# One wait ahead of GpSimd's result scatters, in a cross-attention and top-1 expert kernel

## The reference

```
x = x + tanh(g_xattn) * attention(layernorm(x), ctx, ctx, mask)      # 16 heads of 64
n = layernorm(x)
idx = argmax(softmax(n @ Wg + bg))                                    # one of E = 8 experts
h = gelu(n @ W1[idx] + b1[idx]);  y = h @ W2[idx] + b2[idx]           # 256 -> 256 -> 256
x = x + tanh(g_ffn) * y
```

## Time and profile before

| | |
|---|---|
| median of three timed runs | 210.49 us |
| span of the profiled execution, first to last instruction | 216.8 us |
| the profiled execution's own time | the profile gives its span alone |
| TensorE (PE) matmuls busy | 196.8 us, 91% |
| VectorE (DVE), ScalarE (ACT), GpSimd (POOL) busy | 125.5, 105.5, 89.5 us |
| mean granted TensorE clock | 0.965 |
| scatters to `out` (line 596) | 16, 996 ns mean |
| sort scatters (line 581) | 8, 1006 ns mean |

### The profile page before, as it was taken

The page is one execution under the profiler, slowest core; times in us unless marked ns, Lnnn a source line. Parts: engine busy times, 40 slices in busy tenths (PEclk is TensorE's granted clock), DMA queues, the critical chain, the costliest instruction groups (busy, mean ns, idle before and its releaser), DMA issues.

```text
span 216.8 us, 3994 instructions
## 1 busy us (share of the span) xinstructions
PE 196.8 (91%) x1262; PEld 144.4 (67%) x1262; DVE 125.5 (58%) x526; ACT 105.5 (49%) x377; POOL 89.5 (41%) x129
## 2 busy tenths in 40 slices
PE   7899899799999999999997999989999996399940
PEld 7644576567765546888956667758889994289930
DVE  3896755998893321443279999887343450145420
ACT  3232618799994213022187999976312451135410
POOL 7000632577579600000007997689100057433460
PEclk9999999999999999999999999999999999559995
DMA  5993589999998001900000106000000014520011
GB/s 135 348 385 129 173 315 323 307 287 300 236 216 266 6 0 38 347 1 0 5 0 25 52 26 196 5 0 3 2 0 0 0 52 128 145 72 17 31 52 21
DMA packets 21505, 25.16 MB, mean 116 GB/s; under 512 B 1939, under 2 KB 19805, under 8 KB 21344
## 3 DMA queue, kind: packets, MB, share of 16 engines
q1 hardware_dynamic: 19456, 22.51, 35.2%
q0 software_dynamic: 1152, 2.12, 2.9%
q10 hardware_dynamic: 864, 0.15, 0.4%
HBM read 14.14 MB, written 11.68 MB: 119 GB/s over the span
## 4 chain that ended last, share of the span: by engine, by line
PE 78%; DVE 8%; ACT 5%; issue 4%; DMA 1%; POOL 1%; POOLq 0%; DVEq 0%; ACTq 0%
PE s_bank L1606 13%; PE o_bank L1561 13%; PE s_bank L1906 7%; PE o_bank L1689 7%; PE o_bank L1917 7%; PE t_bank L1663 7%; PE s_bank L1646 6%; PE s_bank L1715 4%; ACT probs L779 4%; PE o_bank L1682 4%; PE s_bank L1895 2%; PE t_bank L1697 2%; DVE probs L1249 1%; PE t_bank L1579 1%; DVE pT L1270 1%
## 5 line engine op out<-in xcount | busy, mean ns | idle before, releaser
L617 POOL TENSOR_TENSOR probs<-probs,r_col 128x512 f32<-128x512 f32 x32 | 33.4, 1043 | 62.1 <-DVE r_col L1260 61.7
L779 ACT ACTIVATE probs<-probs,negm_run 128x160 f32<-128x160 f32 x128 | 53.0, 416 | 5.1 <-DVE negm_run L1249 5.0
L1249 DVE CUSTOM_DVE_ANT_0 probs<-s_bank,maskneg 128x160 f32<-128x160 f32 x128 | 33.2, 318 | 5.8 <-PE s_bank L1646 5.6
L1606 PE MATMUL s_bank<-xnT,wq_sb 128*128 128x512 f32 x64 | 28.8, 598 | 0.5 <-ACT xnT L728 0.5
L1561 PE MATMUL o_bank<-wo_sb,oT 128*128 128x256 f32 x128 | 28.6, 379 | 0.0
L1561 PEld LDWEIGHTS o_bank<-wo_sb,oT 128*128 128x128 f32 x128 | 23.9, 190 | 3.5 <-issue 0.5
L779 ACT ACTIVATION_READ_ACCUMULATOR probs<-probs,negm_run 128x1 f32 x128 | 24.0, 187 | 0.0
L596 POOL DMA_INDIRECT out_dram<-oT x16 | 15.9, 996 | 15.8 <-DVE oT L1198 13.4
L1646 PE MATMUL s_bank<-k_sb,q_sb 64*128 64x160 f32 x256 | 22.3, 311 | 0.0
L1646 PEld LDWEIGHTS s_bank<-k_sb,q_sb 64*128 64x128 f32 x256 | 17.9, 186 | 4.8 <-issue 4.0
L1606 PEld LDWEIGHTS s_bank<-xnT,wq_sb 128*128 128x128 f32 x64 | 11.7, 190 | 13.6 <-issue 13.5
(11 more groups left out here) (155 smaller groups left out, 296.8 us busy)
## 6 DMA issues: line engine op xcount, KB each, us to landing
sorted_rows<-empty_row SPq DMA_DIRECT2D x8, 1040.0 KB, 14.9
oT<-in_L_ffn_W_dram SPq DMA_DIRECT2D x1, 2048.0 KB, 20.0
q_sb<-in_L_ffn_W_dram SPq DMA_DIRECT2D x1, 2048.0 KB, 8.3
oT<-sorted_rows SPq DMA_DIRECT2D x1, 1040.0 KB, 5.4
oT<-sorted_rows SPq DMA_DIRECT2D x8, 130.0 KB, 2.0
wq_sb<-in_L_xattn_Wq_dram SPq DMA_DIRECT2D x2, 512.0 KB, 6.1
mask_sb<-in_mask_BxSxS_bk_dram SPq DMA_DIRECT2D x2, 512.0 KB, 7.1
wk_sb<-in_L_xattn_Wk_dram SPq DMA_DIRECT2D x1, 1024.0 KB, 11.0
```

Source lines behind the costliest of these rows:

```text
L617: nc.gpsimd.tensor_tensor(window_wide(u), window_wide(u), r.rearrange("p i h -> p (i h)") .unsqueeze(2).broadcast_to([P, 4, WIDE]), ALU.mu ...
L779: last = nc.scalar.activation(window_part(u, i, h), window_part(u, i, h), ACT.Exp, bias=negm_run[at], scale=-1.0, accum_out=l_run[at])
L1249: nc.vector.tensor_tensor_reduce(window_part(u, i, h), s_bank[u % 2][:, h, i * CK:i * CK + WK], maskneg[:, q, 0:WK], -SCALE, LARGEST, ALU. ...
L1606: last = nc.tensor.matmul(bank[m % 4], wq_sb[:, c, m * P:(m + 1) * P], xnT[:, c, b * N:(b + 1) * N], start=(c == 0), stop=(c == DC - 1))
```

## The change

More of the change, by code:

```diff
@@ L668, in rest @@
                     scatter(QT + q)
+                pool.wait_ge(experts[1].s_rows[E // 2 - 1], 16)
                 for e in range(E):
```

## The result

The changed kernel takes 213.34 us in the median of four runs (212.84 to 213.72); the kernel before takes 210.48 (210.47 to 210.69, four runs). The ratio is 1.0134, with a 95% interval of 1.0118 to 1.0150: 2.9 us slower. The forecast was 213.0 in a range of 210.4 to 214.8.

The account below looks back on a forecast made before the run. Without the stall, GpSimd's delayed queue was taken to end the changed kernel: last scatter at 205.75 plus 6.5 us gives span 212.2, plus none to all of 1.6 us unexplained; middle 213.0 us, range 210.4 to 214.8.

Parts of the forecast that it names:

- The stall isn't in the timed runs: Late signals and halved clock between passes, from about 181 us; timed runs, 6.3 us below the profiled span, lack it.
- When the wait ends: GpSimd's hold before its first result scatter ends when read 3 of the second pass lands, at 185.6.
- The price of sharing: Second-pass reads beside result scatters: read 3 took 2.7 us against 2.0 alone.
- First scatter: GpSimd's first result scatter starts 0.77 after the wait, at 186.4 instead of 179.90: 6.5 us late.
- The queue of sixteen: GpSimd's result scatters, 1.29 us each: the ninth at 196.7, the sixteenth at 205.75 against 202.4, 3.4 us more.
- What follows the last scatter: Kernel end: 6.5 us from the last scatter's start to the span's end, giving a span of 212.2.
- Around the span: Unexplained time outside the span or left of the stall: between none and 1.6 us, the middle taken.
- What is gained: Start of pass two: reads 0 to 3 have the DMA engines alone; some tenths at most, nothing in the sum.
- My two bounds on its landing: Read 3 of the second pass lands between 185.5 and 186.5.
- The rival built on it (205.9 us): Between the passes: the stall is in the timed runs too and the wait removes it, 205.9 us; chance 0.12.
- Absorbed: Pass two comes late enough that GpSimd's last scatter falls where it did: same time, 210.5 us; chance 0.07.
- The stall moves: Sixteen back-to-back scatters bring the 7.9 us of stall into pass two: 217.6 us; chance 0.04.

Follow-up runs that it names:

- second trace of the kernel before: The kernel before, unchanged, profiled once more for a second look at its trace: 211.02 us, span 209.3, no stall.
- the kernel with the wait after four: Kernel before plus the wait for read 3 of the second pass, placed after four of GpSimd's eight first-pass scatters: 210.75 us, ratio 1.0004.
- The five kernels with the wait moved or the queue cut: Kernel before plus wait for: read 0, 1.0017; read 7, 1.0328; read 3 after four scatters, 1.0004; after two, 1.0008; with half the first-pass scatters omitted, 0.9978.
- the wait for read 7: Kernel before plus a wait for the second pass's last chunk read, ahead of all scatters to the output: 217.37 us, ratio 1.0328.
- the wait for read 0: Kernel before plus a wait for the second pass's first chunk read, ahead of all scatters to the output: 211.07 us, ratio 1.0017.

## Why the prediction was right

*The stall isn't in the timed runs.* Right. I inferred it from 6.3 us that could lie nowhere else; the second trace of the kernel before and the spans of its 46 timed runs show it directly. Without the stall I had put the last scatter at 202.4 and the span at 208.9; the median 210.48 less 1.74 is 208.7.

*When the wait ends.* 185.6 was predicted and it was 185.94: the two turns took 2.20 and 2.12 us, not 2.0 each. The 2.0 came from a single read of the stalled trace, the one issued at 188.32, between two scatters; it was a little too low. The price of sharing that I took from that trace (2.7 us for read 3) was too high: in the second trace of the kernel before read 3 took from 183.85 to 186.10, 2.25 us, and 2.5 in the kernel with the wait after four.

*First scatter.* 186.4 predicted, 186.72 measured; the 0.77 after the wait was 0.78.

*The queue of sixteen.* Right: scatter 9 at 197.09 (196.7 predicted), scatter 16 at 206.12 (205.75), pitch 1.29. The five kernels with the wait moved or the queue cut show it as the cause: the loss comes with the queue and goes with it.

*What follows the last scatter.* This term was mis-sized. I carried over 6.5 us; it was 211.6 - 206.12 = 5.5. It is why the time grew by 2.3 us between the two clean traces (211.02 to 213.34) though the last scatter moved by 3.3. The trace shows where the 1.0 us went: the last scatter landed 3.0 us after its issue and not 4.0. Why it landed sooner stays open (last section).

*Around the span.* I took 0.8, half of what was open; it is 1.74. The errors are +0.4 (late scatters), -1.0 (tail) and +0.9 (around), and the sum came out 0.3 short of the measured 213.34. The path and its waits were right; that the sum is this near is luck, since two errors of about a microsecond each cancel.

*What is gained.* The "some tenths" from read 2 can't be told from the spread: pass two starts 0.35 us sooner than in the one clean trace of the kernel before, but so it does in the kernel with the wait after four. Whatever it is, it is lost behind GpSimd in the change.

The rule of the Trainium skill, page "DMA: Bandwidth & Descriptors", section "Queues, rings and completion order", that the DMA engines take turns between queues, agrees with the traces as far as they go: read 3 took 2.1 us alone and 2.25 and 2.5 beside scatters, a small share. (My two bounds on its landing were 1.0 us apart; the 0.9 in the prediction counts from the 185.6 that I took.) The other rule, page "Runtime: NRT & Kernel Launch", section "The launch sequence", would have put 6.2 us between profile and reported time whatever the kernel. The page speaks of the profile's total time, which no run here gives. For the span the traces don't bear it out: time less span is +1.74 in the changed kernel and +1.7 in the second trace of the kernel before. The rival built on it (205.9 us) fell.

*The rivals on the other side.* "Absorbed" fell since pass two isn't late. "The stall moves" fell: none of the eight later traces has a stall, with up to sixteen scatters back to back beside pass two. My argument against it had a wrong reading, though: I wrote that nothing was late until hidden 7. In the first trace of the kernel before ScalarE's gelu 6 is late already, by 1.0 us (its line there, then in the changed kernel):

```profile
180.50 0.62 ACT L881 ACTIVATE k_sb<-s_bank,b1T 128x128 f32<-128x128 f32 x2 [1.57 <-PE s_bank L1906]
```

```profile
179.55 0.63 ACT L882 ACTIVATE k_sb<-s_bank,b1T 128x128 f32<-128x128 f32 x2 [0.52 <-PE s_bank L1907]
```

Hidden 6 ended at 178.35 + 1.06 = 179.41 there. So the stall began before the first scatter to `out` (179.90) and before SyncE's reads of pass two (181.12), and neither can have started it. The sort scatters that ran at that time ran alike in the eight traces without a stall.

## What to carry to other kernels

A wait in an in-order queue has to be priced by the queue behind it: count what is left to issue, multiply by its pitch, and set it against the moment at which its last item is needed. Here 6.8 us of hold met 3.5 us of slack; two items moved ahead of the wait took almost the whole loss away. The sum gives how late the last item is issued; the time grew by somewhat less, since what followed the last item got shorter. Compare a profile's span with the timed runs before reading it: where it is longer than they are, find the stretch that can't be in them, and do the sums without it.

## What the runs showed of the hardware

The time from the start of the last scatter to the end of the span isn't a constant: 6.5 us in the second trace of the kernel before, 5.5 in the changed kernel, 4.7 with the wait for read 7 (215.7 - 210.97). What changes is the time that the last scatter takes to land: 4.0, 3.0 and 2.3 us after its issue in these three, which leaves 2.5, 2.5 and 2.4. In the last 8.8 us of the kernel before the DMA engines also move instruction blocks. The queues and the median time to landing of the last three scatters there, in its second trace:

```profile
q0 software_dynamic: 144, 0.22, 10.2%
q8 instruction: 3, 0.05, 4.0%
q14 instruction: 7, 0.06, 2.7%
...
out_dram<-oT POOLq DMA_INDIRECT x3, 4.0
```

and in the last 7.6 us of the changed kernel:

```profile
q0 software_dynamic: 170, 0.24, 10.3%
q14 instruction: 3, 0.02, 1.3%
q8 instruction: 1, 0.02, 0.8%
...
out_dram<-oT POOLq DMA_INDIRECT x3, 3.0
```

Ten instruction packets against four, and 4.0 us to landing against 3.0. Counted from the start of the last scatter there are six packets, two, and with the wait for read 7 none. That fits engines which have ended fetching their last code before the last scatters. But the order isn't strict: with the wait for read 0 there are three packets, and the kernel ends 5.0 us after its last scatter starts, sooner than the changed kernel with two. Nothing here changed the fetching alone, so that it is the cause wasn't shown.

What caused the stall in the first trace stays open. From about 179.4 to 188.4 what TensorE had finished was seen by ScalarE and VectorE up to 6.1 us late, and the granted clock, still 1.00 up to 184.5, fell to 0.50 only after TensorE had stood idle from 182.3 on. The lateness began before the scatters to `out`, and it happened in one of the nine executions whose traces are shown. No timed run of the kernel before was above 211.16 us, so none can hold the 7.5 us by which the two spans differ.
